# Wq without its input mean, and half of one softmax sum in four moved from VectorE to GpSimd

## What is computed

```
xn = layernorm(x)                                  # no gain, no shift
k, v = heads(ctx @ Wk.T + bk), heads(ctx @ Wv.T + bv)
q = heads(xn @ Wq.T + bq)
score = einsum('bhij,bhkj->bhik', k, q) / sqrt(8)
attn = softmax(score, axis=1)                      # over the 16 heads, not over the keys
x = x + (einsum('bhik,bhij->bhjk', attn, v) joined over heads) @ Wo.T + bo
h = layernorm(x)
for blk in range(3):                               # weights are dequantised and have a low-rank part
    y = gelu(layernorm(linear(h)) * gamma + beta)
    h = linear(y) + h
out = x + h
```

## Time and profile before

| | |
|---|---|
| time before, median of 3 runs | 396.86 us (396.68 to 397.3) |
| the profiled execution: device time | 397.27 us |
| its span in the trace | 395.5 us |
| PE busy | 355.0 us (90%), 4717 matmuls |
| DVE busy | 345.6 us (87%) |
| ACT busy | 289.6 us (73%) |
| GpSimd busy | 283.1 us (72%) |
| mean granted TensorE clock | 0.982 |

### The profile page before, as it was taken

One profiled execution on the slowest core, in us unless ns is written; L12 is line 12 of the kernel. 1 busy time (PEld: TensorE's weight loads), 2 busy tenths in 40 slices (PEclk: granted clock), 3 DMA queues, 4 the chain that ended last, 5 costly groups with the idle time before them and its releaser, 6 DMA issues.

```text
span 395.5 us, 12974 instructions
## 1 busy us (share of the span) xinstructions
PE 355.0 (90%) x4717; PEld 250.7 (63%) x4717; DVE 345.6 (87%) x863; ACT 289.6 (73%) x542; POOL 283.1 (72%) x349
## 2 busy tenths in 40 slices
PE   2788899999999999999897867789999999999964
PEld 1344566677766676677565645577778877887631
DVE  4618999999999999999999999688999999888852
ACT  3458888888878898788765443557888888888741
POOL 5463998888988898888998787757776667734320
PEclk9999999999999999999999989999999999999995
DMA  5755766558655775458424000000000100110111
GB/s 159 177 172 188 222 189 186 171 180 239 186 162 158 210 217 181 140 177 240 152 88 139 3 0 2 2 1 2 28 28 27 53 27 27 29 53 29 38 44 53
DMA packets 53123, 43.29 MB, mean 109 GB/s; under 512 B 4497, under 2 KB 46945, under 8 KB 53089
## 3 DMA queue, kind: packets, MB, share of 16 engines
q1 hardware_dynamic: 53088, 42.84, 36.0%
HBM read 26.05 MB, written 16.78 MB: 108 GB/s over the span
## 4 chain that ended last, share of the span: by engine, by line
PE 58%; DVE 20%; POOL 8%; issue 7%; ACT 4%; DMA 1%; DVEq 0%; POOLq 0%; ACTq 0%
PE score_ps L983 8%; DVE zsum L554 6%; PE att_ps L948 6%; DVE negmax L533 6%; PE score_ps L888 5%; PE wo_ps L840 5%; PE work L1030 4%; POOL probs L377 3%; PE score_ps L877 3%; PE work L904 3%; PE att_ps L1030 3%; PE score_ps L1030 3%; PE score_ps L976 2%; PE score_ps L834 2%; PE work L908 2%
## 5 line engine op out<-in xcount | busy, mean ns | idle before, releaser
L377 POOL TENSOR_TENSOR probs<-probs,rz 128x1024 f32<-128x1024 f32 x64 | 136.0, 2142 | 27.2 <-DVE rz L557 26.8
L413 POOL TENSOR_TENSOR rs<-ve,minus_half 128x8 f32<-128x8 f32 (+1 forms) x40 | 55.6, 1390 | 53.4 <-DVE ve L520 53.4
L533 DVE TENSOR_REDUCE negmax<-score_ps 128x64 bf16<-128x1024 f32 x64 | 75.3, 1177 | 6.9 <-PE score_ps L877 6.7
L663 ACT ACTIVATE probs<-score_ps 128x1024 f32<-128x1024 f32 x64 | 65.7, 1026 | 18.5 <-PE score_ps L888 18.2
L554 DVE TENSOR_REDUCE zsum<-probs 128x64 f32<-128x1024 f32 x64 | 77.3, 1209 | 1.3 <-ACT probs L663 1.3
L755 ACT ACTIVATE z<-score_ps,nmr,rs 128x128 f32<-128x128 f32 x160 | 60.4, 469 | 15.3 <-POOL nmr L416 15.2
L888 PE MATMUL score_ps<-negmax,ident_bf 128*128 128x512 bf16 x128 | 39.2, 388 | 8.3 <-DVE negmax L533 8.2
L840 PEld LDWEIGHTS wo_ps<-wo_t,att_t 128*128 128x128 f32 x256 | 37.5, 193 | 13.8 <-issue 12.2
L948 PE MATMUL att_ps<-probs,v_diag 128*32 128x64 f32 x2048 | 43.9, 225 | 2.1 <-POOL probs L377 1.9
L983 PEld LDWEIGHTS score_ps<-lin_t,h 128*128 128x128 f32 x320 | 42.1, 192 | 1.3
L983 PE MATMUL score_ps<-lin_t,h 128*128 128x128 f32 x320 | 42.2, 275 | 0.0
(11 more groups left out here) (152 smaller groups left out, 719.9 us busy)
## 6 DMA issues: line engine op xcount, KB each, us to landing
q_parts<-parts SPq DMA_DIRECT2D x16, 512.0 KB, 3.6
q_stack<-q_parts SPq DMA_DIRECT2D x64, 128.0 KB, 3.0
k_stack<-k_parts SPq DMA_DIRECT2D x32, 256.0 KB, 3.3
ctx_sb<-in_ctx SPq DMA_DIRECT2D x16, 256.0 KB, 3.7
k_parts<-parts SPq DMA_DIRECT2D x16, 256.0 KB, 3.0
out<-x_all SPq DMA_DIRECT2D x16, 256.0 KB, 2.3
x_all<-in_x SPq DMA_DIRECT2D x14, 256.0 KB, 3.9
x_all<-in_x SPq DMA_DIRECT2D x1, 512.0 KB, 4.9
```

The lines of the kernel that those rows point to most:

```text
L377: nc.gpsimd.tensor_tensor(e[:, :, :, :], e[:, :, :, :], by_query.broadcast_to([P, BANDS, SEQ, ADJ]), ALU.mult).then_inc(s_probs, 1)
L413: nc.gpsimd.tensor_tensor(rs2[b][:, lo:hi], ve2[b][:, lo:hi], minus_half[:, lo:hi], ALU.pow).then_inc(p_rs[b], 1)
L533: nc.vector.tensor_reduce(negmax[p % 2][:, :], score_ps[p % 2][:, :].rearrange("p (h k) -> p k h", k=SEQ), AX_X, ALU.max, negate=True).the ...
L663: nc.scalar.activation(probs[p][:, :, :, :], score_ps[p % 2][:, :].rearrange("p (u s k) -> p u k s", s=ADJ, k=SEQ), ACT.Exp, scale=SCALE). ...
```

## The change

Two things are done. First, the mean over the input features is taken out of Wq: VectorE sums each row of Wq, scales the sum by -2/128, and writes `wq_c` = 2 Wq - 2 mean; PE transposes that in place of Wq. With it the layer norm of x only has to scale by `half_rstd`, and the bias and its four GpSimd instructions (L387, L393, L402, L403) and their buffers are gone. ACT writes `xln` with Copy and a scale, in place of Identity with a bias and a scale, and waits for the power itself.

Second, for p = 3 of each chunk (`PRE`) GpSimd adds the upper four bands of `probs[3]` to the lower four (`zhalf`, 128x512), right behind mult(2), and VectorE sums the 512 elements of `zhalf` for zsum(3) in place of the 1024 of `probs[3]`.

```diff
+            dve.wait_ge(s_qk_load, 16 * 2)
+            nc.vector.tensor_reduce(wq_sum[:, :], w_in["q"][:, :], AX_X, ALU.add).then_inc(s_wq, 1)
+            dve.wait_ge(s_wq, 1)
+            nc.vector.tensor_scalar(wq_mean[:, :], wq_sum[:, :], -2.0 / D, None, ALU.mult).then_inc(s_wq, 1)
+            dve.wait_ge(s_wq, 2)
+            nc.vector.tensor_scalar(wq_c[:, :], w_in["q"][:, :], 2.0, wq_mean[:, :], ALU.mult, ALU.add).then_inc(s_wq, 1)
...
+                    if p == PRE and live(c):
+                        pool.wait_ge(s_exp, n + 1)
+                        if some(c):
+                            pool.wait_ge(s_zsum, n - PPC + 1)
+                        nc.gpsimd.tensor_tensor(zhalf[:, :, :, :], probs[PRE][:, 0:BANDS // 2, :, :],
+                                                probs[PRE][:, BANDS // 2:, :, :], ALU.add).then_inc(s_zhalf, 1)
                     if p == 1 and live(c + 3):
...
-                        nc.gpsimd.tensor_tensor(agg[:, 0, :], stats[:, :, 1], stats[:, :, 4], ALU.add)
...
-                        nc.gpsimd.tensor_scalar(neg2mean[:, :], agg[:, 0, :], -1.0, None, ALU.mult)
...
-                        pool.wait_ge(s_rstd, c + 4)
-                        nc.gpsimd.tensor_tensor(nmr[:, :], neg2mean[:, :], half_rstd[:, :], ALU.mult)
-                        nc.gpsimd.tensor_scalar(rstd[:, :], half_rstd[:, :], 2.0, None, ALU.mult).then_inc(s_nmr, 1)
...
-                        dve.wait_ge(s_exp, m + 1)
-                        nc.vector.tensor_reduce(zsum[q][:, :], probs[(p - 1) % 4][:, :, :, :].rearrange("p u k s -> p k u s"),
+                        if (p - 1) % 4 == PRE:
+                            dve.wait_ge(s_zhalf, mc + 1)
+                            e = zhalf
+                        else:
+                            dve.wait_ge(s_exp, m + 1)
+                            e = probs[(p - 1) % 4]
+                        nc.vector.tensor_reduce(zsum[q][:, :], e[:, :, :, :].rearrange("p u k s -> p k u s"),
                                                 AX_XY, ALU.add).then_inc(s_zsum, 1)
...
-                            ins = nc.scalar.activation(xln[:, t, :], x_all[:, k, t, :], ACT.Identity,
-                                                       bias=nmr[:, t:t + 1], scale=rstd[:, t:t + 1])
+                            ins = nc.scalar.activation(xln[:, t, :], x_all[:, k, t, :], ACT.Copy,
+                                                       scale=half_rstd[:, t:t + 1])
...
             pe.wait_ge(s_qk_load, 16 * 2)
-            for i, k in enumerate("qk"):
-                nc.tensor.transpose(bank[i][:, 0:P], w_in[k][:, :], ident[:, :]).then_inc(s_tr, 1)
+            pe.wait_ge(s_wq, 3)
+            nc.tensor.transpose(bank[0][:, 0:P], wq_c[:, :], ident[:, :]).then_inc(s_tr, 1)
+            nc.tensor.transpose(bank[1][:, 0:P], w_in["k"][:, :], ident[:, :]).then_inc(s_tr, 1)
```

More of the change, by code:

```diff
@@ L51 @@
 STAGES = 8
+PRE = 3
 EARLY = {0: (12, 3), 1: (13, 3), 2: (15, 0), 3: (16, 0), 4: (16, 2)}
@@ L88, in build @@
         lb_in = sb("lb_in", [P, NLIN, RANK])
+        wq_sum = sb("wq_sum", [P, 1])
+        wq_mean = sb("wq_mean", [P, 1])
+        wq_c = sb("wq_c", [P, P])
         w_t = {k: sb("w_t_" + k, [P, P]) for k in "qkv"}
@@ L111, in build @@
         agg = sb("agg", [P, 4, TPC])
-        neg2mean = sb("neg2mean", [P, TPC])
         veps4 = sb("veps4", [P, TPC])
         half_rstd = sb("half_rstd", [P, TPC])
-        rstd = sb("rstd", [P, TPC])
-        nmr = sb("nmr", [P, TPC])
         xln = sb("xln", [P, TPC, D])
@@ L125, in build @@
         probs = [sb(f"probs{i}", [P, BANDS, SEQ, ADJ]) for i in range(4)]
+        zhalf = sb("zhalf", [P, BANDS // 2, SEQ, ADJ])
         zsum = [sb(f"zsum{i}", [P, SEQ]) for i in range(2)]
@@ L156, in build @@
         s_wperm = sem("s_wperm")
+        s_wq = sem("s_wq")
         s_split = sem("s_split")
@@ L174, in build @@
         s_rstd = sem("s_rstd")
-        s_nmr = sem("s_nmr")
         s_xln = sem("s_xln")
@@ L197, in build @@
         s_zsum = sem("s_zsum")
+        s_zhalf = sem("s_zhalf")
         s_rz = sem("s_rz")
@@ L668, in normalised_input @@
                     if live(k):
-                        act.wait_ge(s_nmr, k + 1)
+                        act.wait_ge(s_rstd, k + 1)
                         if some(k):
```

## The result

The changed kernel takes 427.27 us, median of 4 runs (426.45 to 428.75), against 396.77 us for the kernel before (396.2 to 397.3, 4 runs). The ratio is 1.077 with a 95% interval of 1.0736 to 1.081: slower by 30.5 us. The prediction was 423.7 us, in a range of 418 to 431.

What follows compares the result with a forecast made beforehand. VectorE and PE were taken as full in the attention stage (119.4 and 121.7 of 122 us). Chunks 0 to 11 22.2, chunks 12 to 15 3.5, start 1.1: 26.8 us on 397.27, 424.1; median 423.7, range 418 to 431.

Steps and rivals of the forecast that it cites:

- The wait and the loop: Each chunk, VectorE's zsum(3) waits 2 to 3 us for GpSimd, whose next mult(0) waits for VectorE: a closed cycle.
- the half sum: Term of the cycle: GpSimd's addition of two 128x512 inputs takes 1.04 us, as L434 does.
- The period: Attention stage, mult(0) to next mult(0): 14.50 us a chunk against 12.65, 22.2 us over chunks 0 to 11.
- the scalars: Term of the cycle: GpSimd's layer norm scalars between mult(0) and mult(1) fall from 3.07 to 2.16 us.
- The half zsum: Term of the cycle: VectorE's zsum(3) over 512 elements takes 0.65 us, between bounds of 0.60 and 1.21.
- The start: Before the first scores: first statistics 2.05 us later, first xln about 1.1 us late, all counted: +1.1 us.
- ACT's part: ACT writing xln with Copy and a scale: counted as nothing, ACT being busy 102.7 of 122 us.
- chunk 13: The chunk of the first early step, where GpSimd waits for VectorE's scalars: +0.5 us.
- the smaller terms: The other late parts: chunk 12 at +0.15 us, chunk 14 at +0.7, chunk 15 at +2.1, what follows 0.
- Rival (B): PE's clock falls too: 1 to 2 us once or twice, about 440 us if in every chunk; chance 0.08.
- (C): Half sum in time, PE next limit, period stays 12.65 us, only the start is left: 398 us; chance 0.05.
- (D): Half sum in time, VectorE sheds 0.56 us a chunk, 9.0 in all, less 1.1 at start: 388.8 us; chance 0.03.

Runs made afterwards that it cites:

- e1: The kernel before with only the Wq part of the change, without the half sum: 393.34 us, ratio 0.992.
- e2: The kernel before with only GpSimd's half sum for p = 3 added, without the Wq part: 439.23 us, ratio 1.106.
- e3: The changed kernel with the half sum ahead of mult(2) in GpSimd's stream in place of behind it: 403.44 us, ratio 1.019.
- e6: The changed kernel with one more GpSimd operation of 128x512 elements ahead of each half sum: 446.1 us (one run).
- e5: e1 with VectorE's three instructions on Wq behind the statistics of chunk 0 in place of ahead of them: 391.33 us, ratio 0.987.
- e7: The changed kernel with ten more PE matmuls ahead of shift(0) in chunk 13: 424.75 us, against 426.27 without them on the same chip.
- e10: e1 with VectorE summing only the first 512 of 1024 exponentials for p = 3, no half sum, softmax not right: 390.93 us.
- e11_wq_again: e1 unchanged, run again on the same chip as e10: 392.98 us.

## Why the prediction was right, and where its sum was off

**The wait and the loop: right.** VectorE's wait ahead of zsum(3) was foretold as 2 to 3 us and is 2.67; GpSimd's two waits as about 1.4 each and are 1.43 and 1.39; PE waits 1.2 to 1.4 us for negmax(1), foretold as about 1.3. VectorE's busy share is a miss: I had said 85 to 88% for it as for PE, and it is 81.5% (PE 86.5%), since it also lost half a zsum in each period. e1 and e2 show that the loss belongs to the half sum, e3 that most of it belongs to its place, and e6 that each tenth put in the loop comes out in the period.

**The period: 14.75, not 14.50.** The term that was mis-sized is the half sum, 1.28 for 1.04: I took the row of the same size, but that one reads a broadcast as its second operand, which can account for about half of the error. Two more terms were wrong and nearly cancel: the scalars left 2.26 and not 2.16, because I took off the busy times of L387 and L393 (0.20 and 0.22), where only the distances between starts count (0.15 and 0.18), while the tail saved 0.48 for my 0.49; and the hand-off from GpSimd took 0.03 and not 0.11. The half zsum from the line through two sizes was good: 0.69 for 0.65.

**The start: wrong sign, +1.1 foretold, -2.4 measured.** The step that failed is "what follows is one chain of PE and ACT up to the first scores, so I count all of it". The delay of the first statistics is real (e5: 1.9 us), and the first xln is 0.9 late (1.1 foretold). But behind it the chain runs again through GpSimd's scalars and through ACT's xln of chunk 2, both of which the change shortens, so that the q parts behind it are 1.1 early. I had priced ACT's part at nothing under the cover of its slack in the attention stage, and at the start there is no such cover. A further 1.5 us is PE's clock, which the prediction didn't consider at the start.

**Luck in the total.** The median is 3.6 us above the forecast because the start, 3.5 us too high in the sum, offset nearly half of what the period (3.1), chunk 13 (2.6) and the smaller terms (1.6 together) were too low. With the start forecast rightly the sum would have been 420.2. The mechanism was right; that the total came so near was in part luck.

**Chunk 13: 0.5 foretold, 3.1 measured.** Rival (B) stands in the prediction with this very place, a wait that grows from 2.7 to about 3.4 us (3.54 measured), and a price of 1 to 2 us; it was given a chance of 0.08 and left out of the sum. e7 shows it real at 1.3 to 2.2 us. The forecast wait was already longer than the 3.08 us behind which the clock had fallen, so the sum ought to have had it. In the attention stage a lower clock didn't matter: where it fell there (once, 3.4 us from 46.0, behind a wait of 2.02 us), the period stayed at 14.75, PE having two microseconds to spare. In e6_spare it fell six times between 47 and 177 us, and all periods were 15.84 to 15.89.

**Rivals (C) and (D).** Neither came, since the half sum was not in time. e10 shows what they were worth: with the half sum free, the period goes down by 0.04 and not by 0.56, so (D) was no possible outcome. (C) was right in that the period hardly moves; that PE is what holds it fits the rows and isn't shown.

**ACT.** Copy with a scale takes 0.39 us for 128 elements, mean of 64, where Identity with bias and scale took 0.48. In the attention stage that was covered, as foretold; at the start it wasn't.

## What to carry to other kernels

Before a piece of a saturated engine's work is given to an engine that looks 13% idle, look for where that engine stands in its queue when the result is wanted: here it was 2.3 us behind at that moment, and its idle time lay elsewhere. If the receiver waits in order and the giver later waits for the receiver, the two queues are in series, and every instruction between counts in full, small ones too. Try the relief for free first (leave the work out): if the period doesn't move, something else is at its limit too, and no way of moving that work can shorten the period.

## What the runs showed of the hardware that I had not expected

- A GpSimd sum of two full 128x512 fp32 operands took 1.28 us; at the same place a multiplication with a broadcast operand took 1.16, and elsewhere both a multiplication and a sum with one took 1.04.
- PE's granted clock fell to the lower level behind a wait of 3.54 us, and ten matmuls (2.33 us) in the wait kept it up and made the kernel 1.5 us faster. A shorter wait can do it too, and doesn't always: of two executions of one program, e1_wq_only and e11_wq_again, both with 2.07 us of waiting ahead of the same shift(0), one kept its clock and the other had 0.50 from 195.7 to 198.9, and took 15.25 us for chunk 13 in place of 14.07. In e2_half_only, where PE waited at most 2.04 us ahead of a shift in the attention stage, it fell at 80.0 and 110.7 us behind waits of 1.73 and 1.74, and stayed up behind the same waits at 64 and 142 us.
- VectorE's two-input operations on 128x4 elements ended with the GpSimd operation beside them, 1.75 and 1.23 us long. The Trainium skill (GPSIMD Engine Reference, 8, Key points) names the shared SBUF interfaces; the operations here fit it. VectorE's reductions beside GpSimd's operations kept their durations (zsum of 1024 elements took 1.20 to 1.22).
